# Tile numbers of a graph kernel: from four-number register loads to packed words and steps

## The chip, the cores and the metric

The kernel runs on one core of a Trainium2 chip. The metric is the time on the device in microseconds; before and after are compared by the median of runs on the same chip. Engines are named as in the profile: PE is TensorE's matmuls, PEld its weight loads, DVE VectorE, ACT ScalarE, POOL GpSimd, SP the engine that issues most DMAs. A letter q behind an engine (PEq) means its sequencer, which works through register instructions, waits and branches and hands work to the engine.

## The reference

A graph of 6250 nodes with 256 features and 100000 edges, sorted by destination. Two GATv2 layers with 4 heads are followed by a residual and layer norm, then one GAT layer with 8 heads, again with residual and layer norm. The core of it, shortened:

```python
def _gatv2_layer(x, src, dst, n, Wl, Wr, att, b):
    xl = (x @ Wl).reshape(n, H, C)
    xr = (x @ Wr).reshape(n, H, C)
    e = leaky_relu(xl[src] + xr[dst], 0.2)
    logits = einsum('ehc,hc->eh', e, att)
    m = segment_max(logits, dst, num_segments=n)
    ex = exp(logits - m[dst])
    denom = segment_sum(ex, dst, num_segments=n)
    alpha = ex / (denom[dst] + 1e-16)
    return segment_sum(xl[src] * alpha[:, :, None], dst, num_segments=n) + b
...
x = layernorm(x + gatv2(elu(gatv2(x))))
# third layer: Wh = h W; e = leaky_relu(s1[src] + s2[dst]); softmax over a node's
# incoming edges; sum of attn * Wh[src]
x = layernorm(x + gat(x))
```

## The kernel before

The kernel has four node stages (dense products, layer norm) with three edge stages between them. Nodes are cut into 49 tiles of 128. The sorted edges are cut into chunks of 128, and each chunk is paired with every tile that it touches: 832 items (`ITEMS`), the same for each edge stage. Since edges are sorted, the tile number of an item is that of the item before or one more. Sixteen items (`GI`) make a group, and there are 52 groups (`NG`).

`groups(l, eng, body, state)` (L331) gives every engine the same order of groups: three bodies written out, a loop `Fori(1, NG // 2 - 1)` (L340) of 24 passes of two groups each (`body(j, 1)`, then `body(j + 1, 0)`), and three bodies written out. Ahead of the loop `addr_align(256, max_nops=0)` (L339) puts its first instruction at a multiple of 256 instructions in the engine's program. DVE's loop has 232 instructions, PE's 589 in the first two edge stages. `body` gets three flags: `first` (this group is expanded), `second` (its softmax is worked on), `late` (an earlier group's sums are added).

Who does what in a group of the first two edge stages:

- SP loads the group's one-hot matrix DT, its flags and indices. POOL gathers one block of 128 source rows per item (L692), 16 a group.
- PE expands an item: six bf16 matmuls of DT with the three splits of the tile's features x3 (L1069) and two transposes of the gathered rows (L1075) into pZ. Which tile's features are taken is a register, `tk[i]`. ACT makes the leaky relu (L864), and PE the scores once per four items (L1083).
- ACT copies the logits to cT (L849), DVE scans them for the segment maximum (L1572 and the lines behind it), PE turns carries (L1117), ACT and DVE finish the softmax.
- DVE weighs the gathered rows (L1558) and builds the matrix Dm of the items' destination nodes (L1540). PE multiplies both (L1130) into one of four PSUM banks pS, and DVE adds the bank into the accumulator of the item's tile (L1527), whose place is the register `tq[n]`. DVE's adds follow PE by about four items and are chained by `dve_link`.

In the third edge stage the expansion is L1061, without relu and scores; ACT works on lin and end_row.

The tile numbers come from `t_row`, one row of 832 integers in SBUF which ACT writes ahead of the first node stage (L710). Both engines read it by `load_tiles()`, one TENSOR_LOAD of four consecutive numbers into four registers. In `edge_pe`'s `body` (the trace shows it at L1045) it stands at the start of a group and behind items 3, 7 and 11. In `edge_dve`'s `body` (L1507) it stands at the start and at the end of steps 1, 3 and 4. Step s of DVE's body handles two items: `add(2 * s)`, the matrix Dm, `add(2 * s + 1)`, and the weighing of two rows. At s = 0 the scan of cT follows, at s = 1 that of the row of group ends, at s = 5 the rescaling of one accumulator.

```python
tk.extend(nc.values_load_multi_w_load_instructions(
    t_row[0:1, bass.ds(k0 + len(tk), 4)], engines=(PE,), ...)[1])
...
def add(n):
    dve.wait_ge(seg_done, up(seg_done))
    linked()
    link(v.tensor_tensor(acc_at(n), acc_at(n), pS[:, n % 4, 0:ROW], ALU.add))
```

Of the kernel before, what the change touches and what calls it, by code (L numbers as in the profile page):

```python
# [18 lines left out]
GI = 16  # L19
# [35 lines left out]
def gnn_program(nc, x, src, dst, wl1, wr1, att1, b1, wl2, wr2, att2, b2, w_gat, a_gat, out):  # L55
# [18 lines left out]
    with ExitStack() as ctx:  # L74
        def sb(name, shape, dt=F32):
            return ctx.enter_context(nc.sbuf_tensor(name, shape, dt))
# [4 lines left out]
        def sem(name):  # L81
            return ctx.enter_context(nc.semaphore(name))
# [9 lines left out]
        last_items = sb("last_items", [P, ITEMS], BF16)  # L92
        t_row = sb("t_row", [1, ITEMS], I32)
        ident = sb("ident", [P, P])
# [65 lines left out]
        small = in_g(16, 8).rearrange("p (s b) k -> p s b k", s=4)  # L160
        assert g_at[0] <= 2 * GI * ROW
        xls = sb("xls", [P, 2, ROW])
        pool_pad = sb("pool_pad", [P, 8])
# [49 lines left out]
        pre_idx = sem("pre_idx")  # L213
        pre_acc = sem("pre_acc")

        w_in = sem("w_in")
# [177 lines left out]
        def static(v):  # L394
            return isinstance(v, int)

        def per_h(ap, H):
# [308 lines left out]
        def _(act):  # L706

            act.wait_ge(pre_pe, 2)
            for b in range(NB):
                ins = nc.scalar.activation(t_row[0:1, b * BS:(b + 1) * BS], pX[0:1, b // FB, (b % FB) * BS:(b % FB + 1) * BS], ACT.Copy)  # L710
            ins.then_inc(pre_act, 1)
# [182 lines left out]
        def _(pe):  # L894
# [129 lines left out]
            def edge_pe(l):  # L1024
# [3 lines left out]
                if l < 2:  # L1028
# [5 lines left out]
                settled = {3: wg_done, 4: added, 5: relu_done, 7: scan_done, 9: carry_ready, 10: dif_ready, 11: dt_ready, 12: fx_ready, 13: lin_ready,  # L1034
                           14: logits_copied}

                def body(gh, b, first, second, late):
                    k0 = (gh * 2 + b) * GI
                    c = 1 - b
                    here = pe.snap(landed_need(l, gh)) if first and l < 2 else None  # L1040
                    tk = []

                    def load_tiles():

                        tk.extend(nc.values_load_multi_w_load_instructions(  # L1045
                            t_row[0:1, bass.ds(k0 + len(tk), 4)], engines=(PE,), min_val=0, max_val=TILES - 1,
                            skip_runtime_bounds_check_because="t_k is a tile number by construction")[1])

                    if first:
                        load_tiles()  # L1050

                    def expand(i, freed):

                        if i == 0:
                            pe.wait_ge(dt_ready, up(dt_ready))
# [30 lines left out]
                    for i in range(GI):  # L1086
# [35 lines left out]
                        if at:  # L1122
# [7 lines left out]
                            nc.tensor.matmul(pS[:, i % 4, 0:ROW], Dm[:, i % 8, :], G[:, at[0], at[1], :], start=True, stop=True).then_inc(seg_done, 1)  # L1130
                        if first and i % 4 == 3 and i + 1 < GI:
                            load_tiles()
                        if b == 0 and i in settled:
# [12 lines left out]
        def _(dve):  # L1146
# [3 lines left out]
            def pre(ins, mark=None):  # L1150

                n_pre[0] += 1
                ins.then_inc(pre_v, 1)
                dve.wait_ge(pre_v, n_pre[0])
                assert mark is None or mark == n_pre[0], (mark, n_pre[0])
# [17 lines left out]
            dve.wait_ge(pre_pe, 1)  # L1173
            pre(v.tensor_copy(ki[0:BS, 0, 0:NB], pM[0:BS, 0:NB]))
            pre(v.tensor_copy(kf[0:BS, 0:NB], ki[0:BS, 2, 0:NB]))
            pre(v.tensor_tensor(kf[0:BS, 0:NB], kf[0:BS, 0:NB], pM[0:BS, 0:NB], ALU.subtract), PV_COL)
# [6 lines left out]
            v.memset(end_row[:], -BIG)  # L1183

            def indices(t, b, h):

                if not static(t):
                    return
                if t == OWN:
                    dve.wait_ge(pre_gather, 32 * NB)  # L1190
                    pre(v.tensor_copy(dstf, g_dst))
# [278 lines left out]
            def edge_dve(l):  # L1470
# [25 lines left out]

                up, settle, state = tally()

                def body(gh, b, first, second, late):
                    c = 1 - b  # L1500
                    k0 = (gh * 2 + b) * GI
                    last_group = static(gh) and gh == NG // 2 - 1 and b == 1
                    tq = {}

                    def load_tiles(n):

                        tq.update(zip(range(n, n + 4), nc.values_load_multi_w_load_instructions(  # L1507
                            t_row[0:1, bass.ds(k0 + (n - 3 * GI // 2 - 4), 4)], engines=(DVE,), min_val=0, max_val=TILES - 1,
                            skip_runtime_bounds_check_because="t_k is a tile number by construction")[1]))

                    def acc_at(n):
                        return acc[:, bass.ds(tq[n], 1), :].rearrange("p o r -> p (o r)")

# [14 lines left out]

                    if late:
                        load_tiles(0)  # L1530
                    for s in range(GI // 2):
# [20 lines left out]
                        if at:  # L1552
# [6 lines left out]
                            ins.then_inc(wg_done, 1)  # L1559
                        if late and s in (1, 3):  # L1560
                            load_tiles(2 * s + 2)
                        if second and s == 4:
                            load_tiles(3 * GI // 4)
                        if second and s == 0:
# [117 lines left out]
```

## Time and profile before

| | us |
|---|---|
| median of three runs | 5245.89 |
| the three runs | 5252.4, 5245.89, 5230.47 |
| span of the profiled execution | 5270.5 |
| PE busy in it | 3942.9 (75%) |
| DVE busy | 3296.7 (63%) |
| POOL busy | 2645.7 (50%) |
| ACT busy | 1199.0 (23%) |

The profiled execution is one of its own; its span lies 0.5% above the median of the runs. Busy time counts work of the engines and leaves out register instructions, waits, branches and the issue of DMAs, so a load into a register doesn't appear in it, only in the queries by source line. The three edge stages lie at about 200 to 1765, 1985 to 3575 and 3729 to 5190 us. Matmul ends are modelled; the starts are the better measure.

### The profile page before, as it was taken

The page shows a single profiled execution, that of the slowest core. Times are in us where ns is not written, and L with a number is a line of the kernel's source. Part 1 is how long each engine was busy: PE and PEld are TensorE (multiplying, and loading weights), DVE is VectorE, ACT ScalarE, POOL GpSimd, SP SyncE. Part 2 cuts the span into 40 slices and gives each one's busy share as a digit, 9 for nine tenths or more (in the row PEclk, how much of TensorE's full clock was granted, in tenths as well). Part 3 has the DMA queues.
Part 4 walks back from the last instruction along what each step waited for, and adds up shares of the span by engine and source line. Part 5 has one row for each costly group of instructions (what it writes and reads, how often), then busy time and mean ns, then how long its engine had stood idle before and what let it go on. Part 6 is the DMA issues. An engine that isn't in the chain of part 4 may idle for free. (4 is left out here: it accounts for less than half of the span.)

```text
span 5270.5 us, 122213 instructions
## 1 busy us (share of the span) xinstructions
PE 3942.9 (75%) x31349; PEld 2833.8 (54%) x31350; DVE 3296.7 (63%) x9997; ACT 1199.0 (23%) x4200; POOL 2645.7 (50%) x2941
## 2 busy tenths in 40 slices
PE   6588878888878795888887888787566666666666
PEld 5355555565655574555555556555344444444443
DVE  6466666666666762666666666666466666666666
ACT  3322222222222362222222222223100000000002
POOL 4455555555555224555555555543455555555550
PEclk8799999999899997999999999989777777777779
DMA  3333333333333123333333333325444434343333
GB/s 91 97 95 98 96 98 95 97 93 93 96 96 99 50 66 88 98 94 99 95 98 92 100 94 98 94 77 156 118 110 109 110 106 112 108 111 108 108 106 104
DMA packets 333905, 521.10 MB, mean 99 GB/s; under 512 B 152887, under 2 KB 219617, under 8 KB 333809
## 3 DMA queue, kind: packets, MB, share of 16 engines
q0 software_dynamic: 120320, 338.39, 23.8%
q1 hardware_dynamic: 213489, 181.58, 12.1%
q8 instruction: 42, 0.69, 0.1%
q14 instruction: 54, 0.44, 0.0%
HBM read 484.14 MB, written 35.46 MB: 99 GB/s over the span
## 5 line engine op out<-in xcount | busy, mean ns | idle before, releaser
L692 POOL DMA_INDIRECT gathered<-table,idx x2496 | 2452.7, 983 | 2090.4 <-POOLq L358 1516.7
L1130 PE MATMUL pS<-gathered,Dm 128*128 128x264 f32 x4992 | 1860.0, 456 | 193.2 <-issue 63.0
L1527 DVE TENSOR_TENSOR acc_mem<-acc_mem,pS 128x264 f32 x2496 | 1048.2, 420 | 466.8 <-remote 224.2
L1069 PE MATMUL pZ<-DT,x 128*128 128x128 bf16 x9984 | 1206.0, 229 | 167.1 <-ACT reluT L864 99.3
L1069 PEld LDWEIGHTS pZ<-DT,x 128*128 x9984 | 926.6, 102 | 598.2 <-issue 341.3
L864 ACT ACTIVATE reluT<-pZ 128x256 f32<-128x256 f32 x1664 | 610.2, 382 | 1990.8 <-PE pZ L1075 1248.1
L1130 PEld LDWEIGHTS pS<-gathered,Dm 128*128 128x128 f32 x4992 | 876.0, 218 | 324.5 <-issue 146.8
L1075 PE MATMUL pZ<-ident,gathered 128*128 128x128 f32 x3328 | 972.5, 292 | 18.0 <-issue 10.7
L1558 DVE TENSOR_TENSOR gathered<-gathered 128x256 f32<-128x256 f32 x2496 | 945.8, 419 | 60.6 <-ACT gathered L856 28.8
L1083 PE MATMUL pL<-reluT,attpad 128*32 128x128 f32 x6656 | 277.5, 286 | 408.4 <-ACT reluT L864 373.3
L1540 DVE TENSOR_TENSOR Dm<-pS,rel_items 128x256 f32<-128x256 f32 x1239 | 515.0, 416 | 0.0
L1075 PEld LDWEIGHTS pZ<-ident,gathered 128*128 128x128 f32 x3328 | 495.1, 149 | 20.3 <-issue 10.8
L1061 PE MATMUL pL<-DT,x 128*128 128x128 bf16 x2496 | 350.3, 252 | 136.4 <-ACT first_row L850 100.3
L1061 PEld LDWEIGHTS pL<-DT,x 128*128 x2496 | 257.6, 115 | 345.3 <-issue 246.9
L1083 PEld LDWEIGHTS pL<-reluT,attpad 128*32 128x32 f32 x6656 | 163.2, 111 | 473.8 <-ACT reluT L864 267.5
L1572 DVE TENSOR_TENSOR_SCAN F<-flags,cT 128x128 f32<-128x128 f32 x156 | 66.2, 425 | 548.2 <-ACT cT L849 528.3
L622 POOL TENSOR_TENSOR pool_pad<-zeros 128x1 f32<-128x1 f32 x184 | 56.4, 307 | 396.3 <-DVE gathered L1373 189.5
L975 PE MATMUL pS<-W,gathered 128*128 128x260 f32 (+1 forms) x588 | 177.7, 428 | 38.6 <-ACT gathered L762 36.8
L1577 DVE TENSOR_TENSOR_SCAN Fout<-span_row,end_row 1x68 f32<-1x68 f32 (+1 forms) x156 | 52.1, 334 | 242.2 <-ACT end_row L871 142.5
L1117 PE MATMUL pM<-ident,carry_in 128*128 128x2 f32 x312 | 67.9, 287 | 179.0 <-DVE carry_in L1584 151.3
L1591 DVE SCALAR_TENSOR_TENSOR peak<-flags,pM,peak 128x128 f32<-128x128 f32 x156 | 55.4, 355 | 203.4 <-PE pM L1117 180.3
L1117 PEld LDWEIGHTS pM<-ident,carry_in 128*128 128x128 f32 x312 | 55.1, 221 | 208.9 <-DVE carry_in L1584 157.5
(232 smaller groups left out, 3335.0 us busy)
## 6 DMA issues: line engine op xcount, KB each, us to landing
DT<-rel_dram SPq DMA_DIRECT2D x156, 512.0 KB
gathered<-table,idx POOLq DMA_INDIRECT x2496
flags<-flag_dram SPq DMA_DIRECT2D x1664, 8.0 KB
span_row<-flag_dram SPq DMA_DIRECT2D x1664, 0.1 KB
table<-xls SPq DMA_DIRECT2D x147, 132.0 KB
flags<-flag_dram SPq DMA_DIRECT2D x416, 32.0 KB
gathered<-table SPq DMA_DIRECT2D x98, 132.0 KB, 2.1
gathered<-in_x SPq DMA_DIRECT2D x98, 128.0 KB, 2.1
```

Source lines behind the costliest of these rows:

```text
L692: nc.gpsimd.indirect_dma_start(out=G[:, b, i, :], out_offset=None, in_=tab[l], in_offset=bass.IndirectOffsetOnAxis(ap=idx[:, b, i:i + 1], ...
L864: nc.scalar.activation(relu_slot(i), z_slot(i), ACT.Relu).then_inc(relu_done, 1)
L975: mm = nc.tensor.matmul(pX[:, b, 0:width], hT[:, b, q * P:(q + 1) * P], W[:, q, 0:width], start=(q == 0), stop=(q == 1))
L1061: mm = nc.tensor.matmul(pL[:, 0:P], s3[:, bass.ds(tk[i], 1), s, GI - 1 - i:9 * GI - 1 - i].rearrange("p o c -> p (o c)"), moving, start=(i ...
L1069: mm = nc.tensor.matmul(z_slot(i)[:, half], x3[:, bass.ds(tk[i], 1), s, half].rearrange("p o c -> p (o c)"), moving, start=(s == 0), stop= ...
L1075: mm = nc.tensor.matmul(z_slot(i)[:, half], G[:, b, i, half], ident[:], is_transpose=True, start=False, stop=True)
L1083: nc.tensor.matmul(pL[a * (P // Q):(a + 1) * (P // Q), 0:P], attpad[:, q, ATT0 - k:ATT0 - k + P // Q], relu_slot(Q * k + a)[:, q * P:(q + ...
L1117: nc.tensor.matmul(pM[:, 256:258], carry_in[:], ident[:, 0:33:32], start=True, stop=True).then_inc(carry_turned, 1)
L1130: nc.tensor.matmul(pS[:, i % 4, 0:ROW], Dm[:, i % 8, :], G[:, at[0], at[1], :], start=True, stop=True).then_inc(seg_done, 1)
L1527: link(v.tensor_tensor(acc_at(n), acc_at(n), pS[:, n % 4, 0:ROW], ALU.add))
L1540: ins = v.tensor_tensor(Dm[:, 2 * p % 8:2 * p % 8 + 2, :], numbers.unsqueeze(1).to_broadcast([P, 2, P]), rel.unsqueeze(2).to_broadcast([P, ...
L1558: ins = v.tensor_tensor(gv, gv, row[:, D:D + H].unsqueeze(2).to_broadcast([P, H, D // H]), ALU.mult)
```

## The change

A row of packed words `t_words` of 28 cells x 4 takes the place of `t_row`. A word holds the tile number of a group's first item shifted left by 16, and in the bits below whether the tile number rises from item n to item n + 1. A cell holds PE's two words (columns 0 and 1) and DVE's two (columns 2 and 3). Each engine loads two words with one register load per two groups, at the start of the pass, and takes each next number as the number before plus one bit of the word, by register instructions (`next_tile`) at the place where the item needs it. On DVE that is inside `add(n)`, behind its waits.

ACT now writes the row into `t_of`, which lies in space of the node stage, and waits for DVE first (`pre_v`, `PV_COL`), since DVE has cleared that space. DVE packs the words in seven steps inside the node loop of the first layer (`tile_words`, at tiles `OWN + 10` to `OWN + 16`): one subtraction, four doublings, one that joins numbers and bits, and four strided copies. Three rows of 860 numbers and `t_words` are cleared before. DVE's loop grows from 232 to 275 instructions. The loops' heads stay aligned as they were, and the other engines' programs are the same apart from ACT's copy.

```diff
-        t_row = sb("t_row", [1, ITEMS], I32)
+        CELLS = NG // 2 + 2
+        t_words = sb("t_words", [1, CELLS, 4], I32)
...
+        def load_words(engine, cell, col, n):
+            return list(nc.values_load_multi_w_load_instructions(
+                t_words[0:1, bass.ds(cell, 1), col:col + n].rearrange("p o c -> p (o c)"), engines=(engine,), min_val=0, max_val=(TILES << GI) - 1,
...
+        def first_tile(eng, word):
+            return eng.snap((word >> GI).with_bounds(min_val=0, max_val=TILES - 1))
+
+        def next_tile(eng, word, tile, n):
+            return eng.snap((tile + ((word >> n) & 1)).with_bounds(min_val=0, max_val=TILES - 1))
...
             act.wait_ge(pre_pe, 2)
+            act.wait_ge(pre_v, PV_COL)
             for b in range(NB):
-                ins = nc.scalar.activation(t_row[0:1, b * BS:(b + 1) * BS], ...
+                ins = nc.scalar.activation(t_of[0:1, LEAD + b * BS:LEAD + (b + 1) * BS], ...
...
(edge_pe, body)
-                    if first:
-                        load_tiles()
+                    if first and b == 1:
+                        words[:] = load_words(PE, gh + 1, 0, 2)
+                    elif first and not second:
+                        words[:] = load_words(PE, 0, 0, 2)
+                    word = words[1 - b]
                     def expand(i, freed):
+                        tk.append(next_tile(pe, word, tk[-1], i - 1) if i else first_tile(pe, word))
...
-                        if first and i % 4 == 3 and i + 1 < GI:
-                            load_tiles()
...
(vector, ahead of the first node stage)
+            v.memset(t_of, 0.0)
+            v.memset(step_a, 0.0)
+            v.memset(step_b, 0.0)
+            v.memset(t_words[:], 0)
...
+            def tile_words(step):
+                last = LEAD + ITEMS - 1
+                if step == 0:
+                    dve.wait_ge(pre_act, 1)
+                    words_link(v.tensor_tensor(step_a[:, LEAD:last], t_of[:, LEAD + 1:last + 1], t_of[:, LEAD:last], ALU.subtract))
+                elif step <= 4:
+                    far, span = 1 << (step - 1), WORDS - (1 << step) + 1
+                    frm, to = (step_a, step_b) if step % 2 else (step_b, step_a)
+                    words_link(v.scalar_tensor_tensor(to[:, 0:span], frm[:, far:far + span], float(1 << far), frm[:, 0:span], ALU.mult, ALU.add))
+                elif step == 5:
+                    words_link(v.scalar_tensor_tensor(step_b[:, 0:WORDS - GI], t_of[:, 0:WORDS - GI], float(1 << GI), step_a[:, 0:WORDS - GI],
+                                                      ALU.mult, ALU.add))
+                else:
+                    pairs = NG // 2
+                    for col, cell, at_k, n in ((0, 1, GI + LEAD, pairs), (1, 0, LEAD, pairs), (2, 1, 0, pairs + 1), (3, 1, GI, pairs)):
+                        ins = v.tensor_copy(t_words[0:1, cell:cell + n, col], step_b[:, at_k:at_k + 2 * GI * (n - 1) + 1:2 * GI])
+                    words_link(ins)
...
(edge_dve, body)
+                    if (second or late) and b == 1:
+                        words[:] = load_words(DVE, gh + 1, 2, 2)
+                    word = words[1 - b]
+
+                    def tile_at(n):
+                        if n not in tq:
+                            tq[n] = next_tile(dve, word, tile_at(n - 1), n - 1) if n else first_tile(dve, word)
+                        return tq[n]
                     def acc_at(n):
-                        return acc[:, bass.ds(tq[n], 1), :].rearrange("p o r -> p (o r)")
+                        return acc[:, bass.ds(tile_at(n), 1), :].rearrange("p o r -> p (o r)")
...
-                    if late:
-                        load_tiles(0)
...
-                        if late and s in (1, 3):
-                            load_tiles(2 * s + 2)
-                        if second and s == 4:
-                            load_tiles(3 * GI // 4)
```

## Rows read from the trace of the kernel before

**Rows 1.** The page: span, and the queues that bring instructions (packets, MB, share).

```profile
span 5270.5 us, 122213 instructions
...
q8 instruction: 42, 0.69, 0.1%
q14 instruction: 54, 0.44, 0.0%
```

**Rows 2.** Windows: length, busy PE, PEld, DVE, ACT, POOL; clock, DMA share, GB/s.

```profile
300.00:1700.00 1400.00, 1130.13 (x11068) 833.58 (x11067) 869.02 (x2701) 352.74 (x1233) 743.09 (x760) 0.95 0.35 96
3800.00:5150.00 1350.00, 904.74 (x4422) 600.50 (x4422) 919.88 (x2836) 114.83 (x497) 785.93 (x794) 0.78 0.40 108
```

**Rows 3.** Waits, 300 to 1700 us; last row: 2060 to 3500.

```profile
ACT reluT L864 <- remote: 219.8, 68, 4.7
...
PE pL L1083 <- ACT reluT L864: 149.8, 79, 2.6
...
PE pL L1083 <- ACT reluT L864: 173.7, 88, 3.5
```

**Rows 4.** The loads' two lines: counts, min/median/max ns, first and last start.

```profile
L1045 PEldq TENSOR_LOAD <-t_row x624: 6/332/507, 198.7 to 5146.3; - x156
L1045 PEldq FUSED_REGOPS  x504: 46/46/79, 317.3 to 5116.0; - x168
...
L1507 DVEq TENSOR_LOAD <-t_row x624: 7/344/593, 266.7 to 5177.9; - x156
L1507 DVEq ALU_OP  x360: 40/40/620, 309.5 to 5113.2; - x180
L1507 DVEq FUSED_REGOPS  x216: 5/57/110, 316.2 to 5104.4; - x108
```

**Rows 5.** PE's loads, 2454.5 to 2455 us.

```profile
L1045 PEldq TENSOR_LOAD <-t_row x1: 335/335/335, 2454.7 to 2454.7; - x1
```

**Rows 6.** PE's timeline around that load.

```profile
2453.62 0.61 PE L1130 MATMUL pS<-gathered,Dm 128*128 128x264 f32 x2
2454.06 0.33 PE L1069 MATMUL pZ<-DT,x 128*128 128x128 bf16 x3
...
2454.63 0.61 PE L1130 MATMUL pS<-gathered,Dm 128*128 128x264 f32 x2
2455.26 0.48 PE L1069 MATMUL pZ<-DT,x 128*128 128x128 bf16 x3
```

**Rows 7.** DVE's groups, 60 to 200 us.

```profile
L1203 DVE SCALAR_TENSOR_TENSOR acc_mem<-acc_mem 104x1024 f32<-104x1024 f32 x1 | 1.2, 1212 | 0.0
```

**Rows 8.** DMA queues, 344.5 to 347 us, then 352 to 1720 us.

```profile
q14 instruction: 1, 0.01, 0.8%
...
q8 instruction: 1, 0.02, 0.0%
```

**Rows 9.** Third stage: DVE's first add after a back edge; PE before it.

```profile
4853.15 0.43 DVE L1527 TENSOR_TENSOR acc_mem<-acc_mem,pS 128x264 f32 x1 [1.41 <-issue]
...
4849.45 1.25 PE L1130 MATMUL pS<-gathered,Dm 128*128 128x264 f32 x2 [2.90 <-DVE gathered L1558]
```

**Rows 10.** A DMA issue with its time to landing.

```profile
attpad<-in_L_gnn_att SPq DMA_DIRECT2D x8, 0.2 KB, 2.3
```

**Rows 11.** DVE's timeline after a back edge, second stage.

```profile
2634.85 0.42 DVE L1572 TENSOR_TENSOR_SCAN F<-flags,cT 128x128 f32<-128x128 f32 x1 [5.12 <-ACT cT L849]
```

**Rows 12.** ACT's timeline, and PE's loads, within 200 to 250 us.

```profile
222.50 0.38 ACT L864 ACTIVATE reluT<-pZ 128x256 f32<-128x256 f32 x1 [16.68 <-remote]
...
L1045 PEldq TENSOR_LOAD <-t_row x2: 340/342/343, 207.3 to 248.4; - x2
```

**Rows 13.** ACT's latest relu, 2039 to 2055 us; a window there.

```profile
2054.83 0.38 ACT L864 ACTIVATE reluT<-pZ 128x256 f32<-128x256 f32 x1 [1.09 <-PE pZ L1075]
...
2039.00:2055.00 16.00, 14.87 (x187) 11.04 (x184) 2.46 (x9) 6.45 (x22) 0.00 (x0) 0.97 0.09 28
```

**Rows 14.** ACT's timeline from 1997 us.

```profile
1997.20 0.38 ACT L864 ACTIVATE reluT<-pZ 128x256 f32<-128x256 f32 x1 [3.81 <-remote]
```

More of the change, by code:

```diff
@@ L161, in gnn_program @@
         assert g_at[0] <= 2 * GI * ROW
+        LEAD, WORDS = 3 * GI // 4, ITEMS + 28
+        assert LEAD + GI == 28 and WORDS <= 4 * D and TILES << 16 < 1 << 24
+        t_of, step_a, step_b = (a.rearrange("p a c -> p (a c)")[0:1, 0:WORDS] for a in (own, res, nd))
         xls = sb("xls", [P, 2, ROW])
@@ L214, in gnn_program @@
         pre_acc = sem("pre_acc")
+        words_step = sem("words_step")
         w_in = sem("w_in")
@@ L395, in static @@
             return isinstance(v, int)
+        def load_words(engine, cell, col, n):
+            return list(nc.values_load_multi_w_load_instructions(
+                t_words[0:1, bass.ds(cell, 1), col:col + n].rearrange("p o c -> p (o c)"), engines=(engine,), min_val=0, max_val=(TILES << GI) - 1,
+                skip_runtime_bounds_check_because="a word holds a tile number and 16 bits by construction")[1])
+        def first_tile(eng, word):
+            return eng.snap((word >> GI).with_bounds(min_val=0, max_val=TILES - 1))
+        def next_tile(eng, word, tile, n):
+            return eng.snap((tile + ((word >> n) & 1)).with_bounds(min_val=0, max_val=TILES - 1))
         def per_h(ap, H):
@@ L708, in _ @@
             act.wait_ge(pre_pe, 2)
+            act.wait_ge(pre_v, PV_COL)
             for b in range(NB):
-                ins = nc.scalar.activation(t_row[0:1, b * BS:(b + 1) * BS], pX[0:1, b // FB, (b % FB) * BS:(b % FB + 1) * BS], ACT.Copy)
+                ins = nc.scalar.activation(t_of[0:1, LEAD + b * BS:LEAD + (b + 1) * BS], pX[0:1, b // FB, (b % FB) * BS:(b % FB + 1) * BS], ACT.Copy)
             ins.then_inc(pre_act, 1)
@@ L1035, in edge_pe @@
                            14: logits_copied}
+                words = [None, None]
                 def body(gh, b, first, second, late):
-                    k0 = (gh * 2 + b) * GI
                     c = 1 - b
@@ L1041, in body @@
                     tk = []
[L1043 to L1047, printed above, removed]
-                    if first:
-                        load_tiles()
+                    if first and b == 1:
[3 more added lines that the diff above has]
+                    word = words[1 - b]
                     def expand(i, freed):
+                        tk.append(next_tile(pe, word, tk[-1], i - 1) if i else first_tile(pe, word))
                         if i == 0:
@@ L1183, in _, with words_link @@
             v.memset(end_row[:], -BIG)
+            n_words = [0]
+            def words_link(ins):
+                n_words[0] += 1
+                ins.then_inc(words_step, 1)
+                dve.wait_ge(words_step, n_words[0])
+            def tile_words(step):
[15 more added lines that the diff above has]
+                    words_link(ins)
             def indices(t, b, h):
@@ L1188, in indices @@
                     return
+                if OWN + 10 <= t < OWN + 17:
+                    tile_words(t - OWN - 10)
                 if t == OWN:
@@ L1497, in edge_dve @@
                 up, settle, state = tally()
+                words = [None, None]
                 def body(gh, b, first, second, late):
@@ L1503, in body @@
                     tq = {}
[L1505 to L1509, printed above, removed]
+                    if (second or late) and b == 1:
[5 more added lines that the diff above has]
+                        return tq[n]
                     def acc_at(n):
-                        return acc[:, bass.ds(tq[n], 1), :].rearrange("p o r -> p (o r)")
+                        return acc[:, bass.ds(tile_at(n), 1), :].rearrange("p o r -> p (o r)")
                     def link(ins):
```

## The prediction

> **What bounds the kernel.** I read the page first [rows 1], then stretches by engine [rows 2], then who waits for whom [rows 3]. POOL issues 16 gathers a group, so 760 in 1400 us make 29.5 us a group in the first stage, and 794 in 1350 make 27.2 in the third. Three stages of 52 groups, the second like the first, are then 1533 + 1533 + 1415 us, 85% of the span. No engine fills them: in the first window PE is busy for 1130 of 1400 us, VectorE (DVE) for 869, GpSimd (POOL) for 743; in the third stage PE and DVE are both near 0.67, and the granted clock is 0.78 instead of 0.95. So the bound is a ring of waits: expansion (L1069, L1075), leaky relu on ScalarE (L864), scores (L1083), logits, DVE's scan (L1572), and back through weighing and the freed row slots to the gathers. The reader sees in [rows 3] that ACT waits for signals and PE for relu. In the third stage the ring is another, and PE's weighed matmuls wait for DVE's rows, 2.90 us in [rows 9].
>
> **The register loads as they are.** Each engine makes 624 loads of four numbers, 4 per group, 332 ns each on PE's sequencer and 344 ns on DVE's [rows 4]. Beside them stand 504 address operations of 46 ns on PE, and 360 of 40 and 216 of 57 ns on DVE. They are not engine work; what they cost is what the engine then lacks. One load of PE starts at 2454.7 us and takes 335 ns [rows 5]. Without a load the weighed matmul pair is followed by the next expansion after 0.44 us (2453.62 to 2454.06); across this load it is 0.63 us (2454.63 to 2455.26), and that expansion's first three matmuls take 0.48 us instead of 0.33, because the sequencer is no longer ahead [rows 6]. So 0.19 to 0.34 us shows of it, and part is given back wherever PE waits for relu soon after [rows 3].
>
> **The sum, for one pass of the loop (two groups).** Removed on each engine: 7 of 8 loads. PE: 7 x 0.332 + 7 x 504/624 x 0.046 = 2.6 us. DVE: 7 x 0.344 + 7 x 576/624 x 0.046 = 2.7 us. Added: DVE's loop grows by 43, and 7 loads and 6.5 address operations left it, so some 56 register operations came for 32 tile numbers (a shift, a mask and an add to the number before, 1.75 each). At 46 to 57 ns that is 2.6 to 3.2 us. PE's expansion needs the same numbers, so I take 56 x 0.046 = 2.6 us there. Sequencer time: nil on PE, 0 to +0.5 us on DVE.
> Placement decides the rest. The loads come in lumps; a queue that is ahead swallows a 46 ns step but shows 0.19 to 0.34 us of a load. Against that, the new step of an item stands on DVE behind the wait for seg_done and for the link, so 1.75 x 0.05 = 0.09 us lies in each add of the chain. Both ends: if every load is on the path and every step hidden, 546 x 0.332 = -181 us; if every load is hidden and every step is on the path, 78 x 56 x 0.050 = +218 us. I take 0, since both kinds stand at the same sequencers, which are the shorter reserve only between waits, and the waits of [rows 3] swallow either.
> Ahead of the first stage come 4 memsets of one row, 6 dependent steps of some 850 columns and 4 copies. 1024 columns took 1.21 us [rows 7], so about 1 us each. ACT's copy of the row waits for DVE's column values. Between 0 and 15 us; I take 5. PE's and SP's waits, the DMAs and the order of all other work stay.
> The sum is 0 + 5 us.
>
> **Fetching the longer loop.** The loop's head is put on a boundary of 256 instructions. Queue 14 moved 54 packets and 0.44 MB of instructions, 8 KB each; queue 8, with 42 packets of 16 KB, must be PE's, whose program is the longest [rows 1]. DVE enters its first loop at 309.5 us (its first load with a computed address, ALU_OP in [rows 4]) and makes 24 passes of 59 us. One block of 8 KB comes between 344.5 and 347 us, 0.59 to 0.64 of a pass in, so near instruction 140 of 232; from 352 to 1720 us only queue 8 brings one [rows 8]. I read this as blocks of 128 instructions (estimated from those times and the head's place): entering its second block, DVE fetched the third, and then went back 23 times to the first without a fetch. It holds at least 384 instructions, and 275 lie in three blocks. What stays open is whether the fourth, fetched from the third, then pushes out the first.
> The Trainium skill, "Runtime: NRT & Kernel Launch", section "Instruction fetch mechanics", says otherwise for this change: memory for most engines is two pages of 256 instructions, and a taken branch to a page outside that window stalls until it is fetched. By it each of the 72 back edges could stall; the rows show blocks of half that size and three of them kept, so I leave it at a rival's chance. That page gives TensorE four times the memory, so PE's loop doesn't speak against its rule.
>
> **Rivals.**
> (a) **Steps on the chain, slower.** The 0.09 us stand before all adds while the loads were hidden. In the third stage nothing covers DVE: after the back edge its add comes 1.41 us late for its own instructions (load of 0.346 us included), and PE's matmuls had just waited 2.90 us for DVE's rows [rows 9]. 26 pairs x 32 x 0.09 = +75 us there; half as much in each of the other stages makes 5396 at most, 5321 with the third alone. It decides as soon as an add goes out later than its PSUM bank is wanted. For it: [rows 9]. Against it: 7 loads are gone from the same sequencer.
> (b) **The back edge fetches, slower.** Nearest price is that of a small transfer, 2.3 us from issue to landing [rows 10]. In the first two stages the next adds are followed by 5.12 us of waiting for cT [rows 11], so it is hidden while under that. In the third, 24 x 2.3 to 24 x 4.6 (two blocks one behind another) = +55 to +110 us: 5301 to 5356. It decides if the memory holds three blocks and no fourth. Against it: [rows 8].
> (c) **PE's signals come earlier, faster.** ACT waits 219.8 us in 68 times in the first window for something "remote" [rows 3]: PE had finished and the signal was late. At 207.3 us PE's second load falls among gathers that follow one another, and the relu of 222.50 us starts 16.68 us late [rows 12]; between 2039 and 2055 us, with a group's loads but POOL idle, relu waits 1.09 us at most [rows 13]. If a load amid gathers holds the signals, 7 of 8 causes go. PE's own waits for relu are 149.8 us in 1400 and 173.7 in 1440 [rows 3], so 164 + 185 = 349 over two stages of 1533; 7/8 would be -305, half of that -153: 4941 to 5093. What the third stage would add has no such row, and is left to the range's lower end. Against it: at 1997.20 relu was already 3.81 us late [rows 14], in the early items of a group, ahead of its second load by the order of the program. So gathers alone may do it.
> (d) **Loads were on the path, faster.** If 0.4 us shows of each PE load and half is not given back, 546 x 0.2 = -109, less steps hidden half, +50: about -59, 5187.
>
> **The numbers.** The profiled span is 5270.5 us, the three runs 5230.47 to 5252.4 with a median of 5245.89, so terms taken from it are 0.5% large, which changes none. What measurement can tell from no change is 0.5%, 26 us. Chances: no net change 0.35; (a) 0.16; (b) 0.14; (c) 0.23; (d) 0.12. The likeliest is no net change: 5246 + 0 + 5 = 5251, with its own range 5220 to 5280. To hold 0.8 the range takes (d), the half of (c), (b) and most of (a): 5070 to 5350. (d) gives 0.02 of its chance to "same" and so does (a): faster 0.33, same 0.39, slower 0.28.
>
> **What would show it.** Loads of t_words 78 on each engine. Right: 29.5 us a group in the first stage and 27.2 in the third, ACT's waits for PE and "remote" within a tenth, no 8 KB block inside the loops. (a): more "issue" or "remote" before L1527's successor in the third stage, whose group grows past 27.7 us. (b): 8 KB packets by the dozen on the instruction queue, a gap over 2 us after each back edge. (c): "remote" waits shrink to a third and POOL's waits for its queue with them. The forecast is wrong if the edge stages differ by more than 10 us each.

## The result and the profile after

The changed kernel took 5263.84 us in the median (5258.33 to 5272.06, four runs), the kernel before 5238.18 us (5227.58 to 5252.4). The medians differ by 26 us, a quotient of 1.0049. The ratio on record is 1.0058, with a 95% interval of 1.0036 to 1.0079, so the change made the kernel slower by about half a per cent. That is on the edge of what was called measurable and inside the range of 5070 to 5350. Ratios below are those on record too; they can differ from the quotient of the medians by 0.001.

The pair of profiles can't show 26 us: the profiled execution of before has a span of 5270.5 us, 0.6% above its median, and that of after has 5270.2 us, near its own. They show what changed within. The page of the changed kernel, as [rows 1]:

```profile
span 5270.2 us, 129404 instructions
...
q14 instruction: 56, 0.45, 0.0%
```

There are 7191 more instructions of all kinds, and still 56 packets on the instruction queue, for 54. Nothing is fetched pass by pass. The windows of the first and third edge stage, as [rows 2] (length, busy time of PE, PEld, DVE, ACT, POOL; clock, DMA share, GB/s):

```profile
300.00:1700.00 1400.00, 1120.25 (x11105) 828.75 (x11105) 907.95 (x2714) 353.04 (x1236) 761.61 (x763) 0.96 0.35 96
3800.00:5150.00 1350.00, 920.66 (x4447) 608.79 (x4447) 960.89 (x2844) 115.01 (x497) 794.29 (x796) 0.79 0.40 109
```

The same work gets done in each window to within 0.6% (763 gathers for 760, 796 for 794). DVE is busy 39 and 41 us longer for it, in nearly as many instructions; how that comes about is seen in the third experiment. From 300 to 1700 us, as [rows 3], ACT waits 637.4 us for PE's pZ, where it waited 582.4, and PE 166.5 us for relu instead of 149.8. ACT's wait for a "remote" signal, the one that rival (c) spoke of, is in this window and in that of the second edge stage, 2060 to 3500 us:

```profile
ACT reluT L883 <- remote: 154.1, 48, 4.8
```

```profile
ACT reluT L883 <- remote: 238.8, 73, 4.7
```

Before, they were 219.8 and 216.9 us, so one window shows a fall and the other a rise. Later profiles scatter as widely, with and without the change (see rival (c) below), so neither is an effect of it.

The edge stages, from first gather to last, are 1 to 4 us shorter here than in the profile of before. The forecast had called itself wrong at 10 us each. That sign didn't come, but it tells little, since the profile of before lies 32 us above its median.

The new loads, 27 a stage and engine instead of 208 (81 in all, where 78 were forecast), as [rows 4] (count, shortest/median/longest ns, first and last start):

```profile
L404 PEldq TENSOR_LOAD <-t_words x81: 532/537/714, 202.1 to 5125.4; - x81
L404 DVEq TENSOR_LOAD <-t_words x81: 14/524/776, 215.9 to 5170.2; - x81
```

A load of two numbers takes 537 and 524 ns, one of four took 332 and 344. The first gather starts at 203.7 us, 3.4 us later than in the trace of before; in a later trace of the changed kernel it starts at 201.4 us.

### The profile page after: what moved, and what is told of

It reads as the page before. It is cut to its first block and busy times, and to the rows that moved or that the text cites. A ratio compares the mean times of both kernels' runs of the same rounds, so it can differ in the third digit from the quotient of the medians.

```text
span 5270.2 us, 129404 instructions
## 1 busy us (share of the span) xinstructions
PE 3937.4 (75%) x31349; PEld 2831.9 (54%) x31350; DVE 3422.5 (65%) x10011; ACT 1200.8 (23%) x4200; POOL 2684.8 (51%) x2941
## 5 line engine op out<-in xcount | busy, mean ns | idle before, releaser
L710 POOL DMA_INDIRECT gathered<-table,idx x2496 | 2488.9, 997 | 2046.4 <-POOLq L363 1420.1
L1577 DVE TENSOR_TENSOR acc_mem<-acc_mem,pS 128x264 f32 x2496 | 1063.9, 426 | 539.0 <-remote 200.4
L1086 PE MATMUL pZ<-DT,x 128*128 128x128 bf16 x9984 | 1188.8, 228 | 191.6 <-ACT reluT L883 101.3
L868 ACT ACTIVATE cT<-pL 128x128 f32<-128x128 f32 x156 | 43.3, 278 | 471.0 <-remote 210.2
```

The costliest lines, as they stand in the source:

```text
L710: nc.gpsimd.indirect_dma_start(out=G[:, b, i, :], out_offset=None, in_=tab[l], in_offset=bass.IndirectOffsetOnAxis(ap=idx[:, b, i:i + 1], ...
L1086: mm = nc.tensor.matmul(z_slot(i)[:, half], x3[:, bass.ds(tk[i], 1), s, half].rearrange("p o c -> p (o c)"), moving, start=(s == 0), stop= ...
```

## The experiments

Twelve kernels ran in three series of four, each beside the kernel before. The kernel before took 4023 us in the first series, 5293 us in the second and 4044 us in the third. The second and the third were on the same chip, so this is not a property of a chip. Ratios are therefore always to the kernel before of the same series. I call the series of 4023 and 4044 us quiet. In the other one, as in the first result, PE's signals are late; what is known of the difference stands in the section on the hardware.

### 1 to 4: the parts, and the step ahead of the waits (first series, quiet)

The first kernel keeps both engines' old loads and fills the old row from the new one:

```diff
                 else:
+                    v.tensor_copy(t_row[:], t_of[:, LEAD:LEAD + ITEMS])
                     pairs = NG // 2
...
(edge_pe and edge_dve: load_tiles() as before)
```

> The packed words are built ahead of the first stage and one more copy fills the old row, but both engines keep their four-number loads. The measured change cost 26 us (5238 to 5264). Theory 'steps on DVE's chain': the pre-work is a minor part, 3 to 8 us, so about 5244. Rival 'pre-work': it is the whole loss, 5264.

Measured: 4025.35 us for 4023.08, ratio 1.0008 [0.9999, 1.0018]. The pre-work is worth 2.3 us, with the extra copy in it, and the interval doesn't exclude that it costs nothing. It is a minor part.

The second has the words on PE alone (DVE's `load_tiles()` as before), the third on DVE alone.

> TensorE takes its tile numbers from the words, VectorE by its old loads (loop back at its old length). Theory 'steps on DVE's chain': as with the pre-work alone, 5235 to 5248. Rival 'PE's steps stand where its sequencer is behind': 5255 to 5264. Rival 'fewer PE loads free the late signals': below 5230.

Measured: 4036.06 us, 1.0031 [1.0019, 1.0044]. With PE's steps the kernel takes 10.7 us more than with the pre-work alone. The first theory had given them nothing; they are neither free nor the main part.

> VectorE takes its tile numbers from the words (loop of 275), TensorE by its old loads. Theory 'steps on DVE's chain': the whole loss is here, 5258 to 5270. Rival 'PE's steps': 5240 to 5248.

Measured: 4065.13 us, 1.0106 [1.0091, 1.0121]. With DVE's steps it takes 39.8 us more than with the pre-work alone: most of the loss, where the theory had put the whole of it. The windows from 300 to 1250 us, of the first kernel and of the third, one fence each:

```profile
300.00:1250.00 950.00, 947.58 (x10524) 740.98 (x10524) 810.61 (x2575) 355.91 (x1173) 729.51 (x720) 1.00 0.48 134
```

```profile
300.00:1250.00 950.00, 950.00 (x10398) 732.98 (x10400) 831.00 (x2537) 351.62 (x1161) 704.33 (x713) 1.00 0.48 132
```

In the quiet series PE is busy for all or nearly all of the window and DVE for 0.85 to 0.87 of it. With steps on DVE, PE starts 10398 matmuls where it had 10524, 1.2% fewer.

How a step costs is seen at the end of the first edge stage, where DVE has everything it needs for some microseconds. DVE's timeline with the old loads (first kernel; start, duration, engine and line, operation, count, idle before):

```profile
1313.47 0.42 DVE L1582 TENSOR_TENSOR acc_mem<-acc_mem,pS 128x264 f32 x1
1313.81 0.42 DVE L1595 TENSOR_TENSOR Dm<-pS,rel_items 128x256 f32<-128x256 f32 x1
1314.14 0.42 DVE L1582 TENSOR_TENSOR acc_mem<-acc_mem,pS 128x264 f32 x1
...
1315.15 0.43 DVE L1582 TENSOR_TENSOR acc_mem<-acc_mem,pS 128x264 f32 x1
...
1319.80 0.43 DVE L1582 TENSOR_TENSOR acc_mem<-acc_mem,pS 128x264 f32 x1 [0.21 <-DVE acc_mem L1582]
```

And with the steps (third kernel):

```profile
1329.19 0.42 DVE L1583 TENSOR_TENSOR acc_mem<-acc_mem,pS 128x264 f32 x1
1329.53 0.42 DVE L1594 TENSOR_TENSOR Dm<-pS,rel_items 128x256 f32<-128x256 f32 x1
1329.98 0.43 DVE L1583 TENSOR_TENSOR acc_mem<-acc_mem,pS 128x264 f32 x1
...
1331.00 0.42 DVE L1583 TENSOR_TENSOR acc_mem<-acc_mem,pS 128x264 f32 x1
...
1336.02 0.43 DVE L1583 TENSOR_TENSOR acc_mem<-acc_mem,pS 128x264 f32 x1 [0.37 <-DVE acc_mem L1583]
```

A cycle of two items takes 1.68 us (1313.47 to 1315.15) and with the steps 1.81 (1329.19 to 1331.00). Where adds follow one another alone, 0.43 us of work and 0.21 us idle make 0.64 us, and with the steps 0.43 and 0.37 make 0.80, so a step is worth 0.16 us in the open. The sequencer's records say why. Between the wait for the link and the address operation (FUSED_REGOPS) stand two ALU_OPs of 45 ns, but the second starts 74 ns behind the first and the address operation 77 ns behind the second; the address operation takes 67 ns for 57. So the start-to-start distance counts, and not the duration of 45 ns. In the cycle, the first add's step is hidden behind the work on the rows before it. The second add's shows with 0.12 us: it starts 0.45 us behind Dm (1329.53 to 1329.98), where it started 0.33 us behind it. Dm's record lasts 0.42 us, so the two no longer overlap. That is also why DVE's busy time grows though its work is the same: 0.09 us of overlap for each of 3 x 416 pairs of items would be 112 of the 126 us by which it is longer in the result (an estimate from these rows).

Counted over the stages by DVE's back edges, in the one trace of each kernel: from the first to the last back edge of a stage there are 23 passes of the loop. They take 969.0, 968.7 and 955.8 us in the first kernel and 980.2, 980.3 and 959.4 in the third, which is 11.2, 11.6 and 3.6 us more, 0.49 us a pass in the first two stages and 0.16 in the third. The rest of the span, the groups written out and the node stages, is 12 us longer. Together these are the 38.5 us between the two spans, beside 39.8 between the medians. The ends of the stages belong to that rest: the last add comes 38.3, 42.4 and 33.4 us behind the last gather, for 31.8, 36.0 and 31.6 in the first kernel. Those 15 us can't be added as a whole, because the last gather itself comes sooner behind the last back edge. From the last back edge to the last add it is 3.1, 2.8 and 0.6 us more.

A pass has 16 such cycles. If the 0.12 us showed in each, a pass would be 1.9 us longer (an estimate from these rows); about a quarter of that shows in the first two stages, and less in the third. DVE's waits shrink for the rest. In the window from 300 to 1250 us, 22 to 23 passes long, it waits 50.2 us for cT, where it waited 81.3: 1.4 us a pass. In the third stage, from 2950 to 3850 us, its wait for end_row was in the first kernel and is in the third:

```profile
DVE Fout L1632 <- ACT end_row L891: 34.3, 29, 1.6
```

```profile
DVE Fout L1627 <- ACT end_row L891: 4.9, 8, 0.8
```

Its waits for cT fell from 17.5 to 0.3 us in the same window. So the third stage loses little because DVE had this reserve there, and the steps use it up. The granted clock of that window is 0.95 instead of 0.90, which may make good a further part; that was not tested.

The fourth kernel evaluates the step ahead of the waits:

```diff
                     def add(n):
-
+                        tile_at(n)
                         dve.wait_ge(seg_done, up(seg_done))
```

> The changed kernel with the step of each add moved ahead of its two waits (seg_done and the link), the same instructions in another order, loop still 275. Theory 'steps on DVE's chain': 0.15 us a step leave the chain, so most of the loss goes, 5240 to 5250. Rivals 'pre-work', 'PE's steps' and 'fetch of the longer loop': still 5264.

Measured: 4077.7 us, 1.0134 [1.0119, 1.015]. The experiment did not do what it was meant to: in its trace the ALU_OPs stand behind the link's wait as before, so the compiler put them where the value is used. It is the changed kernel once more, and it says nothing on the place of the steps. The whole change costs 54.6 us here: 2.3 for the pre-work, 10.7 for PE and 39.8 for DVE make 52.8. Its loops take 14.8, 14.7 and 9.1 us more than those of the first kernel, so with both engines' steps the third stage's loop is slower too, and still the least.

### 5 to 8: the change again, the load's length, loads of eight, a longer loop (second series, late signals)

The changed kernel itself:

> The changed kernel itself, beside the kernel before on this chip. The chip of the first four experiments ran the kernel before in 4023 us instead of 5238, and TensorE's signals were not late there. If this is such a chip and the parts add up (pre-work 0.08%, PE 0.23%, DVE 0.98% more): 1.013, about 4075. If moving the step ahead of the waits (1.0134) had helped or harmed, this one stands more than 0.2% off it: above 1.0155 if it helped, under 1.011 if it harmed. If the chip has the late signals (before near 5240): 1.006 again.

Measured: 5319.57 us for 5293.26, 1.0054 [1.0033, 1.0075]. The first result repeats where the signals are late. The cost is 26 us here and 34 to 55 us in the quiet series (the ninth and the fourth kernel).

```diff
-                        words[:] = load_words(PE, gh + 1, 0, 2)
+                        words[:] = load_words(PE, gh + 1, 0, 4)[:2]
...
-                        words[:] = load_words(DVE, gh + 1, 2, 2)
+                        words[:] = load_words(DVE, gh + 1, 0, 4)[2:]
```

> The changed kernel, with each load taking all four words of its cell (16 bytes) instead of two. The two-word loads took 524 and 537 ns, the four-number loads of before 344 and 332. If the length or the alignment of 16 bytes makes the difference, the load falls to about 340 ns and the time by 0 to 0.15% against the changed kernel; if the strided cell or the new row does, it stays above 500 ns, and the time too.

Measured: 5320.67 us, 1.0062 [1.0038, 1.0085]. PE's loads, as above:

```profile
L404 PEldq TENSOR_LOAD <-t_words x81: 327/333/508, 199.2 to 5172.7; - x81
```

Four words from the same cells take 333 ns on PE and 344 ns on DVE, as before the change; two took 537 and 524. The time can't be told from the 5319.57 us of the changed kernel. 81 loads shorter by 0.2 us are 16 us of sequencer time at most, so little was to be seen.

```diff
-                            t_row[0:1, bass.ds(k0 + len(tk), 4)], engines=(PE,), ...
+                            t_row[0:1, bass.ds(k0 + len(tk), 8)], engines=(PE,), ...
...
-                        if first and i % 4 == 3 and i + 1 < GI:
+                        if first and i == 7:
                             load_tiles()
...
-                        if late and s in (1, 3):
-                            load_tiles(2 * s + 2)
-                        if second and s == 4:
-                            load_tiles(3 * GI // 4)
+                        if late and s == 3:
+                            load_tiles(8, 8 if second else 4)
+                        if second and not late and s == 4:
+                            load_tiles(3 * GI // 4, 4)
```

> The kernel before with half as many loads of eight numbers each, no words and no steps. Theory 'steps cost, loads don't': loads were hidden, so within 0.2% of before. Rival 'loads are on the path, the steps cost more than they': 0.3% or more faster than before, as half of the loads go and nothing comes.

Measured: 5283.66 us, 0.9991 [0.9972, 1.0009]. Half as many loads, and no gain that can be told from none. A load of eight numbers takes 591 ns on PE, so the time in loads fell only from 4 x 332 to 2 x 591 ns a group. The kernel tests the number of loads and hardly their time.

```diff
                         if second and s == 0:
+                            for k in range(22):
+                                dve.sem_inc(idle_sem, 1 - 2 * (k & 1))
                             dve.wait_ge(logits_ready, up(logits_ready))
```

> The kernel before with 44 idle additions to an unused semaphore in DVE's loop (22 a group, ahead of the wait for cT), so that the loop has 276 instructions and crosses 256. Theory 'the place of the steps, not the length': no gap after the back edge, the 44 take some 2 us a group mostly inside the wait for cT, 0 to 0.5% slower. Rival 'fetch': an idle gap over 2 us after each back edge and 72 more packets on the instruction queue.

Measured: 5355.73 us, 1.0136 [1.0109, 1.0162]. Slower than the 0 to 0.5% expected, but not by fetching: the instruction queue brings 55 packets in all, for 54 in the kernel before, and DVE's next instruction starts 254 ns behind the back edge (253 before). The additions themselves cost the 62 us, and mostly in one stage. Against the trace of the seventh kernel, whose time can't be told from that of the kernel before, the 23 passes are 7, 12 and 42 us longer in the three stages. In the first two the additions stand ahead of a wait of over 4 us a group. In the third DVE hardly waits for cT (4.6 us in the seventh kernel's trace from 3900 to 5100 us), and with the additions it stands idle there, for instructions of its own ("issue"):

```profile
DVE cT L1571 <- issue: 148.6, 39, 9.0
```

So such work is cheap ahead of a long wait and not free, and dear where that wait is missing. A body used by all stages puts it into each.

### 9 to 12: the steps in one lump, and the limit of the loop (third series, quiet)

> The changed kernel itself once more, as the measure for the next one on the same chip. Where the kernel before runs in 4023 us: 1.0134, as the fourth experiment, whose program turned out to be this one again. Where it runs in 5240 to 5290: 1.0055.

Measured: 4078.29 us for 4044.09, 1.0089 [1.0075, 1.0103]. The changed kernel takes what it took in the first series (4077.7), and its loops agree to 0.1 us; the kernel before is 21 us slower here than there. Why is open. The size of the loss in a quiet series is therefore known only as 34 to 55 us, and its parts only from the first one.

The tenth kernel computes the numbers in registers of their own, where the compiler leaves them, all 16 at s = 0:

```diff
+            held = [dve.alloc_register("held%d" % n) for n in range(17)]
...
-                            tq[n] = next_tile(dve, word, tile_at(n - 1), n - 1) if n else first_tile(dve, word)
+                            before = tile_at(n - 1) if n else None
+                            if n:
+                                dve.reg_alu(held[16], word, n - 1, ALU.logical_shift_right)
+                                dve.reg_alu(held[16], held[16], 1, ALU.bitwise_and)
+                                dve.reg_alu(held[n], held[16], held[n - 1], ALU.add)
+                            else:
+                                dve.reg_alu(held[0], word, GI, ALU.logical_shift_right)
+                            tq[n] = dve.snap(held[n], min_val=0, max_val=TILES - 1)
...
+                        if s == 0 and (late or second):
+                            tile_at(GI - 1)
                         if second and s == 0:
                             dve.wait_ge(logits_ready, up(logits_ready))
```

> The changed kernel with all 16 steps of a group on DVE made in one lump ahead of the wait for cT, in registers of their own, so that the compiler leaves them there; loop 279. Theory 'the steps stand on the chain of adds': the 0.15 us behind each wait go, and DVE's share of the loss (0.98% of 1.34% on the chip of 4023 us, about 0.4% of 0.55% on the other) mostly with them: 1.003 to 1.006, or 1.001 to 1.003. Rival 'it is DVE's sequencer time wherever it is spent': no better than the changed kernel, 1.013 or 1.0055. Rival 'length of the loop': the same.

Measured: 4098.54 us, 1.0136 [1.0121, 1.0152], 20 us slower than the changed kernel. Its timeline has both halves of the answer:

```profile
1332.80 0.43 DVE L1586 TENSOR_TENSOR acc_mem<-acc_mem,pS 128x264 f32 x1 [1.91 <-issue]
...
1334.49 0.42 DVE L1586 TENSOR_TENSOR acc_mem<-acc_mem,pS 128x264 f32 x1
...
1336.17 0.42 DVE L1586 TENSOR_TENSOR acc_mem<-acc_mem,pS 128x264 f32 x1
```

The cycle is back at 1.68 us (1334.49 to 1336.17), so the place of the steps did make the 0.12. But the lump leaves the engine idle for 1.91 us. In the first two stages the wait for cT covers most of it. The 23 passes take 980.8 and 981.2 us there, for 983.9 and 983.3 in the changed kernel. In the third stage the changed kernel has nearly no such wait left (0.8 us from 2950 to 3850 us), and this row of DVE's waits in that window is new:

```profile
DVE cT L1624 <- issue: 67.6, 39, 1.8
```

The 23 passes of the third stage take 988.2 us for 964.9. So 23 us are lost there and 5 won in the others. Neither theory of the expectation comes out clean: the steps off the chain of adds give back a little where a wait takes the lump, and how much of the changed kernel's loss is due to their place alone stays open.

> The kernel before with half as many loads, of eight numbers each (598 ns instead of 344). On the other chip 0.9991. If loads matter where the engines are busy, 0.997 or less on the chip of 4023 us; if they are hidden, 0.999 to 1.001.

Measured: 4056.36 us, 1.0033 [1.0022, 1.0044]. Fewer and longer loads are slower in a quiet series, outside both of the expected ranges. So a load does show there. Whether by its length at one place, more than by the sum, is a guess: a pass of the first two stages takes 42.8 us, for 42.1 with loads of four in the first experiment, but that was another series, and the kernel before itself differs by 21 us between the two. No trace of it with loads of four was kept in this one.

> The kernel before with 328 idle additions to an unused semaphore in DVE's loop: 560 instructions, five blocks of 128. The additions alone take about 15 us a group and slow it much; only the fetching is asked. If DVE holds four blocks (512 instructions), each pass has to fetch again: 100 or more packets of 8 KB on the instruction queue and a gap of 1 us or more behind the back edge, where 276 had 253 ns. If it holds more, none.

Measured: 6344.51 us, mostly for the additions. The instruction queues from 400 to 2000 us, DVE's first stage:

```profile
q14 instruction: 131, 1.07, 0.2%
```

In all there are 490 packets, (490 - 55) / 72 = 6 a pass, and the first instruction behind the back edge starts 3.3 us after it (median of the first two stages) instead of 253 ns. With 560 instructions the loop is fetched anew in each pass; with 276 it isn't.

## Why the prediction was right, and where it was off

**The forecast** was no net change, 5251 us, by 0 for the exchange of loads for steps and 5 for the pre-work. Measured were 5263.84 us, 12.8 us higher and 26 us above the kernel before. The range held it, and so did the narrower one of 5220 to 5280; the case that came true lies on the line between "no net change" and a small form of rival (a). Part of that is luck. Two terms were put at nothing that cost 11 and 40 us in a quiet series, and where signals are not late the same change costs 34 to 55 us, 0.9 to 1.3%, more than what the forecast called no net change. Of its own signs, ACT's "remote" wait was to stay within a tenth and was off by 30% in the first window, which the scatter between profiles explains; its wait for PE (637.4 for 582.4 us) was within a tenth.

**The pre-work**, 5 us: 2.3 us in the first experiment, whose interval also holds no cost at all, and 3.4 us in the first gather of the trace. Right in kind, and if anything too large.

**PE, nil**: 10.7 us in a quiet series. The term that was off is the price of a register operation, taken by its duration of 46 ns. That this is the reason on PE is likely from DVE's rows, and was not tested.

**DVE, 0 to +0.5 us a pass**: this was the term that decided. 39.8 us in a quiet series: 0.49 us a pass in the first two stages, 0.16 in the third, and 12 us outside the loops, which the sum per pass had left out. The 0.09 us a step were worked out as 1.75 operations of 0.05; in the open it is 0.16 (0.64 to 0.80 us), because operations start 74 to 77 ns apart. With 0.075 us for each of its 56 operations the prediction's own sum would have been 4.2 us a pass on DVE, against the 2.7 taken away.

**That the waits swallow either** held in the main. The loops show a quarter or less of the 1.9 us a pass that the steps would cost with no wait, and in the third stage DVE's waits for end_row and cT go with them. Where signals are late the loss is 26 us, where they are not 34 to 55; more waiting to hide in is the likely reason, but the parts were not taken apart in the late series.

**Rival (a)** had the mechanism, steps that stand between an add's wait and the add, but placed it in the third stage, with 75 us. The runs show it the other way round: the third stage's loop lost the least, 3.6 us with DVE's steps alone and 9.1 with both engines', where the first two together lost 22.8 and 29.5. "Nothing covers DVE" there was wrong for single steps, which its waits for end_row and cT took up, and right for a lump of them (the eighth and the tenth experiment). The wait of 2.90 us in [rows 9] was one of 23 such waits of PE, 54.2 us in 1350. And the tenth experiment shows that place is not all: moved out of the chain, the steps cost as much elsewhere.

**Rival (b)**, the fetch, did not occur: 56 packets for 54, and 253 ns behind the back edge. The changed kernel's queue brings one packet between 360 and 380 us, at the end of the first pass, and none from there to 1720 us. The reading of [rows 8], three blocks kept, was right, and what it left open is answered: the fourth block doesn't push out the first.

**Rival (c)**, loads that hold PE's signals: refuted. The first experiment has all 624 loads of each engine, and from 300 to 1250 us ACT's longest row of waits is this:

```profile
ACT reluT L884 <- PE pZ L1095: 466.0, 631, 1.6
```

No relu waits more than 1.6 us, and no row of that whole trace is "remote", where the kernel before had waits of 4.7 us in [rows 3]. Where signals are late, the loads don't matter either. With all or half of the loads, ACT's "remote" part ahead of relu is 219.8, 249.7 and 261.0 us in the first window and 216.9, 220.2 and 245.7 in the second stage's (the kernel before, the seventh and the eighth). With an eighth of them it is 154.1, 242.8 and 223.5, and 238.8, 246.7 and 257.6 (the first result, the fifth and the sixth).

**Rival (d)**, loads on the path, -59 us: the seventh experiment, half of the loads, brought 0.9991. That is no gain that can be told from none, but the time in loads fell by a ninth only, so it is a weak test. Stronger are the second and third experiments: 7 of 8 loads went from one engine and the kernel was slower each time, so what the loads cost was less than what the steps do.

No kernel of these beats the one before by more than the measurement leaves open.

## What to carry to other kernels

Price a register operation by the distance from its start to the next one's (here 74 to 77 ns, so 0.15 to 0.16 us for the two operations of a step behind a wait), not by its duration of 45 ns, and count it wherever the engine has no slack, the ends of a stage included. A register load of several numbers was the cheaper way: 332 ns for four numbers, 83 each, against 0.15 us for the step of one. Ask of each stage which wait would hide the work: the same 22 additions a group cost 7 to 12 us in a stage with a wait at that place and 42 in one without. A rare sight in one timeline, such as one long wait in the third stage, doesn't name the bound of a stage: the waits summed over it say more. And one window of one profile isn't an effect: the "remote" waits ranged from 154 to 261 us with no bearing on the change.

## What the hardware showed that was not expected

**Two speeds of the same program.** The kernel before took 5238 and 5293 us beside the first result and in the second series, and 4023 and 4044 us in the first and third; 5293 and 4044 are from the same chip. In the longer executions PE's signals arrive late in bursts while gathers run: ACT's waits ahead of relu have a "remote" part of 219.8 us with single ones of 4.7 us, [rows 3], while in the quiet window shown above those for PE's pZ don't exceed 1.6. The granted clock of the whole execution is 0.88 to 0.90 in the one and 0.94 to 0.96 in the other, the kernels with idle additions left out. DMA moves 96 GB/s in the one and 134 in the other, as it must when a pass of the same work takes 59 us or 42. What else ran on the chip isn't visible in a trace of one core, so the cause stays open. A comparison across series would have been off by 30% (5238 to 4023).

**Two numbers take longer to load than four.** 537 ns on PE for the two numbers in the first half of a cell and 524 on DVE for those in the second, 333 and 344 ns for four, 591 and 598 for eight. Whether the length or the place of the two counts wasn't tried apart.

**How much of a loop DVE keeps.** Its instructions come as single packets of 8 KB, read above as blocks of 128 instructions. Loops of 232, 275, 276 and 279 instructions are not fetched again; one of 560 is, with 6 packets and 3.3 us a pass. So at least the three blocks of a loop and the one fetched ahead stay, and not the five blocks of the long loop and one more. The Trainium skill, "Runtime: NRT & Kernel Launch", section "Instruction fetch mechanics", gives most engines 32 KiB, or 512 instructions, and that size agrees with both sides. It also says that this is two pages of 256, and there the traces differ: the packets come one by one at half that size, and no back edge of a loop of 275, whose end lies in the second page, was followed by a fetch.
